# Selective-scan stage: fp32 input rows, a re-ordered preparation, three state buffers, and another write order of the exponentials

## The reference

```
xn    = rmsnorm(layernorm(x))
proj  = xn @ x_proj_w.T              # 8 low-rank numbers, 64 of B, 64 of C per token
delta = softplus(low_rank @ dt_proj_w.T + dt_proj_b)
A     = -exp(A_log)                  # 128 channels x 64 states
for 64 steps t, in 32 chunks of 64 tokens at once:      # 2 sequences x 16 chunks
    h = exp(delta_t * A) * h + delta_t * xn_t * B_t     # h: 128 x 64 per chunk
    y = sum over states of h * C_t
out   = (y + xn * D) @ out_proj_w.T
```

## Time and profile before

| | us |
|---|---|
| median of 3 runs (1643.6 to 1648.71) | 1644.42 |
| profiled execution, its own time | 1653.65 |
| its span | 1651.6 |

### The profile page before, as it was taken

One profiled execution on the slowest core, in us unless ns is written; L12 is line 12 of the kernel. 1 busy time (PEld: TensorE's weight loads), 2 busy tenths in 40 slices (PEclk: granted clock), 3 DMA queues, 4 the chain that ended last, 5 costly groups with the idle time before them and its releaser, 6 DMA issues.

```text
span 1651.6 us, 30294 instructions
## 1 busy us (share of the span) xinstructions
PE 1370.3 (83%) x11160; PEld 917.5 (56%) x11160; DVE 1037.8 (63%) x2050; ACT 958.5 (58%) x1507; POOL 649.1 (39%) x520
## 2 busy tenths in 40 slices
PE   4889996699999987889999996714888888877998
PEld 2667774344444434657666774413666666655676
DVE  5887766877777755786675445513666666665533
ACT  4667773166666676767675442534677677653433
POOL 2756656711222003756553002503566666661000
PEclk9999998699999997999999998755555555557999
DMA  4100000000000000010000000134111101110000
GB/s 139 53 25 1 0 1 1 1 1 2 2 0 1 1 1 26 26 53 1 0 1 1 1 0 0 21 69 73 46 26 25 25 22 25 31 53 1 1 0 25
DMA packets 34316, 32.20 MB, mean 19 GB/s; under 512 B 24200, under 2 KB 27672, under 8 KB 32536
## 3 DMA queue, kind: packets, MB, share of 16 engines
q1 hardware_dynamic: 34200, 30.64, 7.5%
HBM read 24.81 MB, written 5.82 MB: 19 GB/s over the span
## 4 chain that ended last, share of the span: by engine, by line
PE 56%; DVE 14%; ACT 13%; issue 8%; SPq 5%; POOL 2%; DMA 1%; DVEq 0%; POOLq 0%; ACTq 0%
PE ps L595 12%; PE ps L672 7%; PE ps L895 7%; PE ps L682 7%; ACT arena L1149 6%; PE ps L787 4%; PE ps L750 4%; PE ps L868 3%; PE ps L770 3%; DVE maxima L1667 3%; ACT hr L1038 2%; DVE xn L1468 2%; SPq L505 2%; PE ps L881 1%; SPq L499 1%
## 5 line engine op out<-in xcount | busy, mean ns | idle before, releaser
L1149 ACT ACTIVATE arena<-ps 128x512 f32<-128x512 f32 x256 | 244.5, 1080 | 116.4 <-PE ps L868 116.1
L1387 POOL TENSOR_TENSOR arena<-arena 128x512 f32<-128x512 f32 x126 | 223.4, 1793 | 194.9 <-PE ps L895 83.8
L1667 DVE TENSOR_REDUCE maxima<-ps 128x1 f32<-128x512 f32 (+3 forms) x320 | 190.3, 633 | 59.4 <-PE ps L753 39.9
L868 PE MATMUL ps<-arena 12*128 12x64 bf16 x2048 | 136.5, 236 | 101.0 <-DMA arena<-dt_parts 52.8
L595 PE MATMUL ps<-xp,wup 128*128 128x512 f32 (+1 forms) x768 | 207.8, 418 | 13.9 <-ACT hr L1038 10.0
L1411 POOL TENSOR_TENSOR hr<-arena,hr 128x512 fp32r<-128x512 f32 x128 | 173.7, 1363 | 93.8 <-ACT hr L1038 93.6
L595 PE MATMUL ps<-hr,wdn 128*128 128x512 f32 x768 | 201.3, 412 | 8.8 <-DVE hr L1570 7.3
L1104 ACT ACTIVATE arena<-ps 128x1024 f32<-128x1024 f32 (+1 forms) x192 | 150.5, 812 | 73.2 <-PE ps L770 37.0
L1038 ACT ACTIVATE arena<-ps 128x512 f32<-128x512 f32 x256 | 162.5, 635 | 51.0 <-PE ps L595 50.6
L868 PEld LDWEIGHTS ps<-arena 12*128 12x128 bf16 x2048 | 103.7, 121 | 157.1 <-ACT arena L1149 77.1
L595 PEld LDWEIGHTS ps<-xp,wup 128*128 128x128 f32 x768 | 148.3, 200 | 64.3 <-POOL wup L1398 16.4
(11 more groups left out here) (206 smaller groups left out, 2162.6 us busy)
## 6 DMA issues: line engine op xcount, KB each, us to landing
arena<-up_dram SPq DMA_DIRECT2D x16, 256.0 KB, 2.9
arena<-dn_dram SPq DMA_DIRECT2D x16, 256.0 KB, 3.2
arena<-up_dram SPq DMA_DIRECT2D x2, 1024.0 KB, 4.9
arena<-dn_dram SPq DMA_DIRECT2D x2, 1024.0 KB, 7.8
b_parts<-arena SPq DMA_DIRECT2D x16, 96.0 KB
dt_parts<-arena SPq DMA_DIRECT2D x8, 192.0 KB
u_parts<-arena SPq DMA_DIRECT2D x16, 96.0 KB
arena<-dt_parts SPq DMA_DIRECT2D x32, 48.0 KB
```

Of the source, the lines that this page charges most:

```text
L868: mm = e.matmul(ps[:, 4 + n % 2, j * 64:(j + 1) * 64], aw[32 * r:32 * r + KR, g0 + j, :], dts[k % 2][32 * r:32 * r + KR, g0 + j, :, th * T ...
L1149: e.activation(to.rearrange("p t m d -> p d m t"), ps[:, 4 + n % 2, :].rearrange("p (d m t) -> p d m t", d=DBK, t=TU), ACT.Exp, scale=-1.0 ...
L1387: e.tensor_tensor(hs[:, t % 2, cols], decay[:, u % 2, t4 * W + cols.start:t4 * W + cols.stop], hs[:, 1 - t % 2, cols], ALU.mult).then_inc( ...
L1667: e.tensor_reduce(maxf[:, at_max[0]:at_max[-1] + 1:max(1, at_max[-1] - at_max[0])], ps[:, n % 2, 0:ng * w].rearrange("p (g k) -> p g k", g ...
```

## The change

1. **fp32 rows.** u and B are no longer split. They stay fp32; `inputs` multiplies 2 rows (one a sequence) of fp32, 16 matmuls a step as before. B is computed by TensorE directly into padded rows of 128 (`rows_b`, with a new padded weight `xpb`).
2. **Few large stores.** B goes out in 4 DMAs, u in 8, each when its blocks are ready; delta for steps 0 to 7 in one, the rest in one. Loads of u and B cover 4 steps (8 DMAs), loads of delta 8 steps (12 DMAs) and are apart. Loads for steps 0 to 3 go ahead of the stores of the rest of delta.
3. **Preparation.** GpSimd clears two areas in the stage before and has no part in the preparation; VectorE subtracts the parts of delta; the blocks of 512 tokens are interleaved on TensorE and ScalarE; the skip product (`xd`) comes last.
4. **Three state buffers.** The multiplication of step t waits for the output of step t - 3.
5. **Exponentials.** `decay_bank` reads its bank with the 8 channels innermost (64 fp32 apart in PSUM) and writes 8 neighbouring fp32.

```diff
+TI = 4
+NI = NSTEP // TI
...
-decay = carve(2 * TU * W).rearrange("p (u n) -> p u n", u=2)
-hs = carve(2 * W).rearrange("p (s n) -> p s n", s=2)
...
 czf = carve(2 * TU * NM * 32)
 cz = czf.rearrange("p (s j n) -> p s j n", s=2, j=4)
 aw = carve(GD * P // 2).bitcast(BF16).rearrange("p (g n) -> p g n", n=P)
+dts0 = carve(GD * NM * TC // 2)
+decayf = [carve(TU * W) for _ in range(2)]
+hsf = [carve(W) for _ in range(3)]
+us1 = carve(TI * 4 * D)
+bs1 = carve(TI * 4 * P)
 assert top[0] <= kept
...
+zt, xd, soft, lof = [decayf[0][:, n * T:(n + 1) * T] for n in range(4)]
...
+uTf, bfull = decayf[1][:, 0:T], decayf[1][:, T:2 * T]
...
-sp.wait_ge(SC["zeroed"], 3)
+sp.wait_ge(SC["zeroed"], 2)
...
-def store_b(k):
+def store_b(b):
     for m2 in range(2):
-        p0 = m2 * CHUNK + k * TC
-        sp.dma_start(scratch["b"][k][:, :, m2::2].rearrange("a b h t n -> t a (b h) n"),
-                     bparts[p0:p0 + TC].rearrange("t a i c n -> t a i (c n)")).then_inc(parts_out, 16)
-def store_u(k):
+        sp.dma_start(scratch["b"][:, b, m2::2, :],
+                     bT[m2 * CHUNK:(m2 + 1) * CHUNK, 8 * b:8 * b + 8, :]).then_inc(b_out, 16)
+def store_u(g):
     for m2 in range(2):
-        p0 = m2 * CHUNK + k * TC
-        sp.dma_start(scratch["u"][k][:, :, m2::2].rearrange("a b h t d -> t a (b h) d"),
-                     uparts[p0:p0 + TC]).then_inc(parts_out, 16)
-def store_dt(k):
-    sp.dma_start(scratch["dt"][k].rearrange("a b d n -> d (a b) n"),
-                 dtparts[:, k].rearrange("p a b n -> p (a b) n")).then_inc(parts_out, 16)
-def fetch(k):
+        m0 = g % 2 * 8 + m2
+        sp.dma_start(scratch["u"][:, g // 2, m0:m0 + 7:2, :],
+                     uT[m2 * CHUNK:(m2 + 1) * CHUNK, TPB * g:TPB * (g + 1), :]).then_inc(u_out, 16)
+def store_dt(k0, k1):
+    sp.dma_start(scratch["dt"][k0:k1].rearrange("k a b d n -> d (k a b) n"),
+                 dtparts[:, k0:k1].rearrange("p k a b n -> p (k a b) n")).then_inc(dt_out, 16)
+def fetch_inputs(k):
+    for r in range(RG):
+        rows = slice(32 * r, 32 * r + B)
+        sp.dma_start(usf[k % 2][rows].rearrange("p (t n) -> p t n", t=TI),
+                     scratch["u"][TI * k:TI * (k + 1), :, 4 * r:4 * r + 4, :].rearrange(
+                         "t b m d -> b t (m d)")).then_inc(u_in[k % 2], 16)
+        sp.dma_start(bsf[k % 2][rows].rearrange("p (t n) -> p t n", t=TI),
+                     scratch["b"][TI * k:TI * (k + 1), :, 4 * r:4 * r + 4, :].rearrange(
+                         "t b m n -> b t (m n)")).then_inc(b_in[k % 2], 16)
+def fetch_dt(k):
     for c0, na in RUNS:
         for r in range(RG):
             rows = slice(32 * r + 2 * c0, 32 * r + 2 * c0 + 2 * na)
             sp.dma_start(dtsf[k % 2][rows], scratch["dt"][k, 0:na, :, GD * r:GD * (r + 1)].rearrange(
                 "a b d n -> (a b) (d n)")).then_inc(dt_in[k % 2], 16)
...
-sp.wait_ge(SC["b_split"], 1)
-for k in range(NC):
-    store_b(k)
-sp.wait_ge(SC["dt_split"], 4)
-store_dt(0)
-sp.wait_ge(SC["u_split"], 4)
-store_u(0)
-sp.wait_ge(parts_out, 16 * (2 * NC + 3))
-fetch(0)
-for k in range(1, NC):
-    store_dt(k)
-    store_u(k)
-sp.wait_ge(parts_out, 16 * 5 * NC)
-fetch(1)
-for k in range(2, NC):
-    sp.wait_ge(SC["in_done"], 3 * TC * (k - 1))
-    sp.wait_ge(SC["spread_done"], 2 * BKU * (k - 1))
-    fetch(k)
-sp.wait_ge(SC["in_done"], 3 * TC * (NC - 1))
+for b in range(B):
+    sp.wait_ge(SC["bf_ready"], 2 * b + 2)
+    store_b(b)
+for g in range(NTB):
+    sp.wait_ge(SC["uT_ready"], g + 1)
+    store_u(g)
+sp.wait_ge(SC["dt_split"], NTB)
+store_dt(0, 1)
+sp.wait_ge(b_out, 16 * 2 * B)
+sp.wait_ge(u_out, 16 * 2 * NTB)
+fetch_inputs(0)
+sp.wait_ge(dt_out, 16)
+fetch_dt(0)
+store_dt(1, NC)
+sp.wait_ge(dt_out, 32)
+fetch_inputs(1)
+sp.wait_ge(SC["xn_turned"], NTB)
+fetch_dt(1)
+for k in range(2, NI):
+    sp.wait_ge(SC["in_done"], 3 * TI * (k - 1))
+    fetch_inputs(k)
+    if k % 2 == 0 and k // 2 + 1 < NC:
+        sp.wait_ge(SC["spread_done"], 2 * BKU * (k // 2))
+        fetch_dt(k // 2 + 1)
+sp.wait_ge(SC["in_done"], 3 * TI * (NI - 1))
...
-k = t // TC
-if t % TC == 0 and 0 in banks:
-    e.wait_ge(u_in[k % 2], 16 * KR * (k // 2 + 1))
-    e.wait_ge(b_in[k % 2], 16 * KR * (k // 2 + 1))
+k = t // TI
+if t % TI == 0 and 0 in banks:
+    e.wait_ge(u_in[k % 2], 16 * RG * (k // 2 + 1))
+    e.wait_ge(b_in[k % 2], 16 * RG * (k // 2 + 1))
 for mm_ in range(4):
     for r in banks:
-        rows = slice(32 * r, 32 * r + KR)
-        mm = e.matmul(ps[:, r, mm_ * D:(mm_ + 1) * D], bs[k % 2][rows, mm_, t % TC, :],
-                      us[k % 2][rows, mm_, t % TC, :], start=True, stop=True)
+        rows = slice(32 * r, 32 * r + B)
+        mm = e.matmul(ps[:, r, mm_ * D:(mm_ + 1) * D], bs[k % 2][rows, t % TI, mm_, :],
+                      us[k % 2][rows, t % TI, mm_, :], start=True, stop=True)
...
+def turn_rows(g):
+    e.wait_ge(SC["xr_ready"], TPB * (g + 1))
...
+def rows_b(g):
+    for i in range(TPB * g, TPB * (g + 1)):
+        half = STATE * (1 - i // 8)
+        mm = e.matmul(ps[:, 4 + g, i % TPB * P:(i % TPB + 1) * P], ut[:, i * P:(i + 1) * P],
+                      xpb[:, half:half + P], start=True, stop=True)
+    mm.then_inc(SC["bc_done"], 1)
+turn_rows(0)
+turn_rows(1)
+low_rank(0)
+turn_rows(2)
+low_rank(1)
+steps_of(0)
+turn_rows(3)
+low_rank(2)
+steps_of(1)
+low_rank(3)
+steps_of(2)
+rows_b(0)
+rows_b(1)
+steps_of(3)
+rows_b(2)
+rows_b(3)
+for h in range(2):
+    e.wait_ge(SC["bf_ready"], h + 1)
...
+    mm.then_inc(SC["bc_done"], 1)
+for g in range(NTB):
+    e.wait_ge(SC["z_added"], g + 1)
+    for j in range(TPB):
+        mm = e.transpose(ps[:, g, j * P:(j + 1) * P], xn[:, TPB * g + j, :], ident[:])
+    mm.then_inc(SC["xn_turned"], 1)
+for g in range(NTB):
+    e.wait_ge(SC["u_ready"], g + 1)
+    if g < 2:
+        e.wait_ge(SC["cT_ready"], g + 1)
+    else:
+        e.wait_ge(SC["bf_ready"], g + 1)
+    for j in range(TPB):
+        mm = e.transpose(ps[:, 4 + g, j * P:(j + 1) * P], ut[:, (TPB * g + j) * P:(TPB * g + j + 1) * P], ident[:])
+    mm.then_inc(SC["u_turned"], 1)
+e.wait_ge(SC["uT_ready"], NTB)
...
-    e.wait_ge(SC["prep_done"], 1)
+    e.wait_ge(SC["skip_done"], 1)
 if q == 0 and u == 1:
-    e.wait_ge(parts_out, 16 * 2 * NC)
+    e.wait_ge(b_out, 16 * 2 * B)
+    e.wait_ge(u_out, 16 * 2 * NTB)
 if q == 0 and u >= 2:
     e.wait_ge(SC["multiplied"], TU * (u - 1) - 1)
     e.wait_ge(SC["pool_multiplied"], YP * (TU * (u - 1) - 1))
 e.wait_ge(SC["spread_done"], n + 1)
-to = decay[:, u % 2, :].rearrange("p (t m d) -> p t m d", t=TU, d=D)[:, :, :, d0:d0 + DBK]
-e.activation(to.rearrange("p t m d -> p d m t"),
-             ps[:, 4 + n % 2, :].rearrange("p (d m t) -> p d m t", d=DBK, t=TU), ACT.Exp,
+to = decayf[u % 2].rearrange("p (t m d) -> p t m d", t=TU, d=D)[:, :, :, d0:d0 + DBK]
+e.activation(to, ps[:, 4 + n % 2, :].rearrange("p (d m t) -> p t m d", d=DBK, t=TU), ACT.Exp,
              scale=-1.0).then_inc(SC["decay_ready"], 1)
...
+rows_copy(0)
+rows_copy(1)
+low_copy(0)
+rows_copy(2)
+low_copy(1)
+rows_copy(3)
+low_copy(2)
+low_copy(3)
+b_copy(0)
+soft_exp(0)
+b_copy(1)
+soft_exp(1)
+c_copy(0)
+b_copy(2)
+soft_exp(2)
+c_copy(1)
+b_copy(3)
+soft_exp(3)
+    dt_cast(0, g, "dt_ready", "dt_first")
+    dt_cast(1, g, "dt_rest1", "dt_second")
+    e.copy(uTf[:, g * TB:(g + 1) * TB], ps[:, 4 + g, :]).then_inc(SC["uT_ready"], 1)
+    dt_cast(2, g, "dt_rest2", "dt_split")
+for g in range(NTB):
+    e.wait_ge(SC["xn_turned"], g + 1)
+    e.activation(xd[:, g * TB:(g + 1) * TB], ps[:, g, :], ACT.Copy,
+                 scale=dskip[:, 0:1]).then_inc(SC["xd_ready"], 1)
+e.wait_ge(SC["cT_ready"], 2)
...
-e.wait_ge(SC["arena_free"], 1)
-e.memset(bparts, 0.0).then_inc(SC["zeroed"], 1)
-e.memset(aw, 0.0).then_inc(SC["zeroed"], 1)
-e.memset(czf, 0.0).then_inc(SC["zeroed"], 1)
-e.wait_ge(SC["bf_ready"], 1)
-for b in range(B):
-    i0 = b * NT // B
...
-        ins = e.tensor_copy(part, full)
-        if a < NPART - 1:
-            pool_chain(ins)
-            pool_chain(e.tensor_tensor(full, full, part, ALU.subtract))
-ins.then_inc(SC["b_split"], 1)
...
-        e.tensor_tensor(dt_piece(g), dt_piece(g), dt_part(n, g), ALU.subtract).then_inc(SC[done], 1)
...
-    if t >= 2 and n == 0:
-        e.wait_ge(SC["y_done"], t - 1)
+    if t >= 3 and n == 0:
+        e.wait_ge(SC["y_done"], t - 2)
...
+def relu_mixture_pool(e, st, nxt):
+    if nxt and nxt["kind"] == "scan":
+        e.wait_ge(MX["y_read"], len(gelus) * NTB * E)
+        e.memset(czf, 0.0).then_inc(SC["zeroed"], 1)
+        e.memset(aw, 0.0).then_inc(SC["zeroed"], 1)
...
+    dt_rest(0, g, "dt_first", "dt_rest1")
+for g in range(NTB):
+    dt_rest(1, g, "dt_second", "dt_rest2")
...
-for g in range(NTB):
...
-    link(e.tensor_tensor(rest, ps[:, 4 + g, :], parts[0], ALU.subtract))
-    link(e.tensor_copy(parts[1], rest))
-    link(e.tensor_tensor(rest, rest, parts[1], ALU.subtract))
-    e.tensor_copy(parts[2], rest).then_inc(SC["u_split"], 1)
-e.wait_ge(SC["u_split"], NTB)
...
```

(59 more changed lines are left out.)

149 lines of the change are left out of this document (52 added, 97 removed).

## The result

The changed kernel takes 1794.8 us (1793.4 to 1796.9, 4 runs) against 1645.39 (1643.6 to 1648.71, 4 runs): a ratio of 1.091 (95% interval 1.0885 to 1.0928). It is 9.1% slower, where 1630 us was forecast. Its profiled execution took 1795.51 us with a span of 1793.4; before, 1653.65 and 1651.6. The spans differ by 141.8 us.

What follows compares the result with a forecast made beforehand. Dependent work queued on TensorE and ScalarE was taken to set the pace: 1653.65 - 28.8 (preparation) - 18 (early stall) + 32 (steady steps) + 1 (last steps) = 1640, less 9.2 from profiled to median: 1630 us; range 1515 to 1720.

Steps and rivals of the forecast that it cites:

- Inputs: Steady steps: fp32 row groups run side by side, only bank 3's matmuls delay the output; +1.3 us a step, 5.2 a period.
- Rival 3: Inputs: fp32 weight loads show, about 1720 us; all 32 of a step one after the other, about 1780; chance 0.17.
- Exponentials: Steady steps: writing runs of 8 neighbours saves 0.42 us each, seven times in a four-step period, -2.9 us.
- Rival 2: Exponentials stay at 1.08 us because the spaced PSUM read pays a penalty; about 1671 us; chance 0.15.
- Rival 1: Scan: TensorE's clock rises above 0.50, shortening outputs; 17.7 us a period, about 1519 us; chance 0.20.
- Preparation: Before the scan's steps: four terms bring the first spread to about 1073, -28.8 us (bounds -18 to -36).
- the clearing's term: Preparation: GpSimd's clearing moves to the stage before and no longer slows a small VectorE instruction; -8.1 us.
- Rival 4: Preparation doesn't come forward since large stores or loads land late; half of -47 lost, about 1654 us; chance 0.10.
- The early stall: Start of the scan, step 3's wait for loads: goes but for a microsecond, -18 us (bounds -10 to -19).
- Three buffers: State buffers: worth 0 in 56 of 60 steps; in the last four, longer inputs eat the freed wait, +1 us.

Runs made afterwards that it cites:

- experiment 6: The changed kernel with all 32 input instructions of a step issued in one run going round the four row groups: 1670.17 us, ratio 1.013.
- experiment 1: The changed kernel with the row groups of the spreads moved on by one: 1723.08 us, ratio 1.044.
- experiment 2: The changed kernel with inputs multiplying only the upper bf16 halves of the fp32 rows, lower-half products left out: 1568.84 us, ratio 0.950.
- experiment 10: The changed kernel with the twelve bf16 rows of u and b back and the rest of the change kept: 1594.48 us, ratio 0.967.
- experiment 5: The changed kernel with the inputs of banks 2 and 3 issued together, alternating between their row groups: 1696.81 us, ratio 1.028.
- experiment 3: The kernel before the change with only the new write order of the exponentials: 1615.33 us, ratio 0.979.
- experiment 9: The kernel using only the upper bf16 halves of u and b, with two state buffers in place of three: 1571.37 us, ratio 0.954.

## Why the prediction was wrong, by its steps

- **The step that failed is "Inputs"**: "if fp32 row groups also run side by side, banks 0 to 2 are hidden ..., but bank 3's matmuls stand between the third spread and the output in each step: +1.3 us, 5.2 in a period". They can run side by side (experiment 6), but not in this order. Bank 2 and bank 3 are issued as runs of one row group, whose eight starts take 1.7 us; what is behind them gets ahead of the last few only (1.4 us, experiment 1), and where a spread of the same row group comes next, the next run begins 2.1 us behind. Bank 3's part by itself was right: 2.00 us up to the output, where 1.9 was forecast. But three runs lie on the path and not one; measured, +14.8 us a period. The steady steps take 172 us more where +32 was forecast, 140 of the 155 us that the sum missed. The sign of the case hung on it: without the four-byte inputs the kernel is faster (experiments 2 and 10).
- The price of one run was in the rows: an output's four to a column group in 1.86 us, and 0.19 us for a weight load. 1.7 us was measured. What was missing was not a duration but who stands behind whom: the order of issue in a step is written out in the kernel, and reading it against row groups would have shown it. The bf16 ones hid the same order, since four of them take 0.4 to 0.6 us. The Trainium skill (TensorE: Matmul & The Clock Gate, section "The mechanism") says that matmuls start and end strictly in program order, and that a weight load overlaps running matmuls only where the row group differs. The traces agree with the first in the main, but an instruction of another row group can start a little early: the input at 1302.96 starts before the last of the spread ahead of it (1303.01), and in experiment 1 six instructions were passed at once. The ends in the trace are modelled and show nothing of it. With the second they don't agree, as it is put: within one row group 0.213 us did not shrink when the load or the stream alone was halved, and fell to 0.113 with both, so the two overlap there.
- **Rival 3** gave in its last form a step of 8.7 us and 1780 us, near the 8.61 and 1794.8 measured, by another mechanism: it had all 32 weight loads one after the other. Experiments 5 and 6 refute that, with 32 in 2.2 us. It was left outside the range, and that was the second mistake: its number was the only one in which the runs did not overlap, and nothing in the rows excluded it.
- **Exponentials**: -0.42 each was forecast, -0.487 measured. Alone they gave -2.4 a period of -2.9 forecast, and 37 us in all. In the changed kernel they give nothing in the steady steps, since the forecast took ScalarE for the pace and the inputs had become it. **Rival 2** is out: the Trainium skill (SBUF — State Buffer, section "Door 1: The DMA port swizzle") has a price for each move to another line, 8 bytes in PSUM, but ScalarE's reads 256 bytes apart show none here: 0.596 us, where an eviction of neighbours takes 0.665.
- **Rival 1**: the clock stayed at 0.50, with TensorE busy without a break for 318 us.
- **Preparation**: first spread at 1077.92 (forecast 1073), 24.2 us earlier of 28.8. The second step that failed is here: "In the stage before, GpSimd has nothing else to do". The small VectorE instruction beside the clearing went from 8.25 to 0.17 us, but the clearing now holds one of the stage before. The first row is of the kernel before, the others of the changed one:

```profile
894.53 0.18 DVE L1511 TENSOR_SCALAR rank<-rank 128x32 f32<-128x32 f32 x1
892.76 3.51 POOL L1460 MEMSET arena<- 128x4096 f32 x1
895.08 4.68 DVE L1548 TENSOR_SCALAR rank<-rank 128x32 f32<-128x32 f32 x1
1023.19 0.87 DVE L1482 BATCH_NORM_STATS2 stats<-x 128x6 f32<-128x128 f32 x4 [0.18 <-DVE x L1652]
```

  The instruction ends with the second clearing (896.21 + 3.51), as the one of the earlier trace rows did, and that part of the stage lasts 53.5 us from one norm to the next where it lasted 49.0. It is 53.5 in all twelve kernels with the moved clearing and 49.0 in experiment 3, which has the old one. So the scan stage begins 4.5 us late (1023.19; 1018.70 before), and the clearing's term is -3.6 and not -8.1. Within the stage the first spread comes 28.7 us earlier: 15.1 up to ScalarE's last cast (17.5 forecast), 8.8 from it to the store (8.8), 4.5 from the store to the loads (2.5) and 0.3 from these to the spread. **Rival 4** is out.
- **The early stall** went: no wait for the later deltas in the profile. From step 2 to step 3 it is 6.85 us with short inputs (experiment 2), where it was 25.5: 18.6, as forecast. The first spread comes 22.9 us earlier there and the output of step 3 another 24.0, since the first steps are shorter too; with 28.8 and 18 forecast, the two misses cancel. With the four-byte inputs the 24.0 is 10.6.
- **Three buffers**: nothing in the steady part, as said. In the last steps they free 0.95 us where inputs are short (experiment 9), but the four-byte ones take more: 5.9 us a step against 4.41, forecast 4.7.
